# Three fp32r products instead of one fp32 product in an FFN, and layer-norm variances on VectorE

## The reference

```python
def _feature_map(x): return jax.nn.elu(x) + 1.0
# 1: linear attention, 16 heads of 16
q = _feature_map((n @ Wq + bq).reshape(B, S, H, Dh)); k = _feature_map(...); v = ...
kv = jnp.einsum('bkhd,bkhm->bhdm', k, v)
out = jnp.einsum('bqhd,bhdm->bqhm', q, kv) / normalizer[..., None]
x = x + out.reshape(B, S, D) @ Wo + bo
# 2: FFN with a shared expert, and routed ones
out_shared = _sq_relu(xf @ Ws1) @ Ws2            # 256 -> 128 -> 256
# 3: attention over the first 16 tokens of each batch, three iterations; every other row gets only the bias ob
out = attn_out @ ow.T + ob
# 4: the same FFN as in 2, with the same weights, on the new x
```

## Time and profile before

| | |
|---|---|
| median of 3 runs | 400.91 us |
| the profiled execution | 400.6 us |
| its span | 398.7 us |
| mean granted clock of PE | 0.992 of full speed |
| second pass, first to last L1163 | 182.93 to 378.46 us |

### The profile page before, as it was taken

How to read it: one execution, slowest core, us unless ns; L and a number is a source line. 1 busy time by engine, 2 the same in 40 slices (tenths; PEclk the granted TensorE clock), 3 DMA queues, 4 the chain that set the end, 5 groups by cost and what they waited for, 6 DMA issues and landing times.

```text
span 398.7 us, 7260 instructions
## 1 busy us (share of the span) xinstructions
PE 373.1 (94%) x2458; PEld 306.7 (77%) x2458; DVE 297.6 (75%) x677; ACT 234.2 (59%) x402; POOL 249.7 (63%) x305
## 2 busy tenths in 40 slices
PE   8879999999999999988879999999999998989993
PEld 4778989998999899876758887687667766677762
DVE  5688786778677866785696559887787879885574
ACT  3587776777677767544444755356454554364451
POOL 3388885788578855579373536787465845955302
PEclk9999999999999999999998999999999999999998
DMA  8831111111100000032530321233223321331103
GB/s 258 249 102 53 54 53 54 54 53 54 55 0 2 0 2 0 19 92 93 163 98 23 109 76 65 88 109 110 57 70 99 111 80 36 108 110 57 48 10 113
DMA packets 29625, 29.79 MB, mean 75 GB/s; under 512 B 5750, under 2 KB 25468, under 8 KB 29564
## 3 DMA queue, kind: packets, MB, share of 16 engines
q1 hardware_dynamic: 29004, 28.51, 23.3%
q10 hardware_dynamic: 560, 0.52, 0.5%
HBM read 19.98 MB, written 8.98 MB: 73 GB/s over the span
## 4 chain that ended last, share of the span: by engine, by line
PE 63%; DVE 18%; issue 7%; POOL 7%; ACT 3%; DMA 1%; DVEq 0%; POOLq 0%; ACTq 0%; SPq 0%
PE PB L1585 6%; DVE ln_bn L1109 5%; PE PA L1655 3%; PE PG L1436 3%; PE PA L1661 3%; PE PA L1656 3%; PE PG L1431 3%; PE PG L1432 3%; PE PT L1345 2%; PE PT L1632 2%; DVE x_all L1163 2%; DVE x_all L1171 2%; POOL o_lo L535 2%; PE PB L1390 2%; PE PA L1390 2%
## 5 line engine op out<-in xcount | busy, mean ns | idle before, releaser
L535 POOL TENSOR_TENSOR o_lo<-q_all,o_hi 128x512 fp32r<-128x512 f32 x32 | 40.2, 1279 | 33.5 <-ACT o_hi L811 33.5
L518 POOL TENSOR_TENSOR xn_pair<-scratch,xn_pair 128x512 fp32r<-128x512 f32 x32 | 41.9, 1308 | 30.6 <-ACT xn_pair L654 30.6
L1585 PE MATMUL PB<-ws,scratch 128*128 128x256 f32 x240 | 58.8, 388 | 1.6 <-DVE x_all L1171 1.5
L1585 PEld LDWEIGHTS PB<-ws,scratch 128*128 128x128 f32 x240 | 44.2, 192 | 15.4 <-issue 10.6
L1109 DVE BATCH_NORM_STATS2 ln_bn<-x_all 128x6 f32<-128x256 f32 x128 | 44.9, 413 | 0.9
L511 POOL TENSOR_TENSOR x_all<-x_all,wvo 128x1024 f32<-128x1024 f32 x16 | 45.3, 2833 | 0.0
L527 POOL TENSOR_TENSOR q_all<-q_all,scratch 128x512 f32<-128x512 f32 x32 | 41.3, 1313 | 0.0
L818 ACT ACTIVATE scratch<-PB,ln_rsq 128x256 f32<-128x256 f32 x28 | 11.7, 470 | 41.1 <-issue 25.9
L935 DVE TENSOR_TENSOR o_lo<-scratch,o_hi 128x512 fp32r<-128x512 f32 x32 | 32.8, 1024 | 4.1 <-ACT o_hi L672 2.7
L1431 PE MATMUL PG<-xn_pair,o_hi 128*128 128x256 f32 x128 | 32.1, 285 | 2.0 <-ACT o_hi L672 2.0
L647 ACT ACTIVATE scratch<-x_all,ln_shift,ln_rstd 128x255 f32<-128x255 f32 x60 | 31.0, 596 | 4.0 <-POOL ln_shift L507 4.0
(11 more groups left out here) (283 smaller groups left out, 1101.3 us busy)
## 6 DMA issues: line engine op xcount, KB each, us to landing
scratch<-inv_scratch SPq DMA_DIRECT2D x32, 256.0 KB
x_all<-n_L_attn_a_inputs_q_dram SPq DMA_DIRECT2D x15, 512.0 KB, 3.5
out_dram<-x_all SPq DMA_DIRECT2D x15, 512.0 KB, 5.7
inv_scratch<-inv_turned SPq DMA_DIRECT2D x16, 32.0 KB
out_dram<-x_all SPq DMA_DIRECT2D x2, 256.0 KB, 2.3
x_all<-n_L_attn_a_inputs_q_dram ACTq DMA_DIRECT2D x2, 128.0 KB, 2.8
x_all<-n_L_attn_a_inputs_q_dram SPq DMA_DIRECT2D x2, 128.0 KB, 2.9
setup<-in_L_attn_a_Wq_dram ACTq DMA_DIRECT2D x1, 256.0 KB, 4.9
```

The lines of the kernel that those rows point to most:

```text
L518: nc.gpsimd.tensor_tensor(halves[:, :, 1, :], pair(xn[n % 2], h), halves[:, :, 0, :].bitcast(F32), ALU.subtract).then_inc(x_lo, 1)
L535: nc.gpsimd.tensor_tensor(o_lo[:, c, :], q[:, c, :], o_hi[:, c, :].bitcast(F32), ALU.subtract).then_inc(o_lo_done, 1)
L1585: last = mm(four(dst)[:, t, :], h[:, t * P:(t + 1) * P], ws2[:, :], start=(t % 2 == 0 and not onto_rows), stop=True, skip_group_check=True)
```

## The change

The folded product and the first down projection become three fp32r products each. ACT makes `h2_hi` from `h2s` behind `lay_ob`, POOL `h2_lo` behind its addition L622, and `ws2` and `wc` are split once, in step 0. PE takes the high products behind the output product, and the low ones behind `chain(i, 3)`. The variances move from POOL to the end of DVE's step, with the reciprocal; the inverse norm stays at the head of DVE's next step. Two of the four statistics of L1163's result now stand behind the additions L1171. The second down projection stays fp32, and waits for each of its PSUM banks by itself.

```diff
@@ gpsimd, step
-                if runs(r) or runs(v):
-                    ge(pool, rsq, i - 1)
-                    variances(i, r, v)
                 if 1 <= i < B:
                     scale_query(i + 1)
                 chain(i, 1)
...
                     nc.gpsimd.tensor_tensor(last, last, y3[:, by_dve(v):T, :], ALU.add).then_inc(out_pool, 1)
+                if runs(r):
+                    pool.wait_ge(h2_hi_done, r + 1)
+                    ge(pool, f2_mm, 2 * r)
+                    nc.gpsimd.tensor_tensor(h2_lo[:, :], h2s, h2_hi[:, :].bitcast(F32), ALU.subtract).then_inc(h2_lo_done, 1)
                 chain(i, 2)
                 if i + 1 < NG:
                     query_low(i + 1)
@@ scalar, fold_ffn and fold_ffn_product
+                nc.scalar.activation(ws2_hi[:, :], ws2[:, :], ACT.Copy).then_inc(ws2_hi_done, 1)
...
-                nc.scalar.activation(wc, PT[:, 0, 0:F], ACT.Copy).then_inc(fold_sb, 1)
+                act.wait_ge(bo_added, NG)
+                nc.scalar.activation(wc_hi[:, :], PT[:, 0, 0:F], ACT.Copy).then_inc(fold_sb, 1)
@@ scalar, step
                     lay_ob(i, r, v)
+                    act.wait_ge(f1_scaled, r + 1)
+                    ge(act, f2_mm, 2 * r)
+                    nc.scalar.activation(h2_hi[:, :], h2s, ACT.Copy).then_inc(h2_hi_done, 1)
@@ vector
-            def reciprocal_variances(i, r, v):
...
+            def inverse_variances(i):
+
+                slots = slice(0 if runs(i) else 1, 2 if runs(i - 1) else 1)
+                a, d, both = ln_a[:, slots, :], ln_d[:, slots, :], ln_bn[:, slots, :, :]
+                ge(dve, rsq, i)
+                if runs(i):
+                    dve.wait_ge(bn2, T * (i + 1))
+                if runs(i - 1):
+                    dve.wait_ge(bn3, T * i)
+                nc.vector.tensor_tensor(d, both[:, :, :, 1], both[:, :, :, 4], ALU.subtract).then_inc(var, 1)
+                nc.vector.tensor_tensor(a, both[:, :, :, 2], both[:, :, :, 5], ALU.add).then_inc(var, 1)
+                dve.wait_ge(var, 5 * i + 1)
+                nc.vector.tensor_tensor(d, d, d, ALU.mult).then_inc(var, 1)
+                dve.wait_ge(var, 5 * i + 2)
+                nc.vector.tensor_scalar(a, a, 4.0 / D, 4.0 * LN_EPS, ALU.mult, ALU.add).then_inc(var, 1)
+                dve.wait_ge(var, 5 * i + 4)
+                nc.vector.tensor_tensor(a, a, d, ALU.add).then_inc(var, 1)
+                dve.wait_ge(var, 5 * i + 5)
+                ge(dve, r2_mm, i)
+                if runs(i - 1):
+                    ge(dve, f4_scaled, act_tiles(i - 1))
+                nc.vector.reciprocal(ln_rsq[:, slots, :], a).then_inc(rsq, 1)
@@ vector, step
+                    dve.wait_ge(ws2_hi_done, 1)
+                    nc.vector.tensor_tensor(ws2_lo[:, :], ws2[:, :], ws2_hi[:, :].bitcast(F32), ALU.subtract).then_inc(wc_lo_done, 1)
                 if i + 2 < NG:
                     inverse_norm(i + 2)
-                if runs(r) or runs(v):
-                    reciprocal_variances(i, r, v)
...
-                    x_stats(n, 0, bn2)
+                    x_stats(n, 0, bn2, (0, 1) if runs(r) else range(T))
                 if runs(r):
...
                                                 ALU.add).then_inc(f2_added, 1)
+                if runs(i) and runs(r):
+                    x_stats(n, 0, bn2, (2, 3))
                 chain(i, 3)
...
+                if i <= NG:
+                    inverse_variances(i)
@@ tensor
-            def down(dst, h, done, onto_rows):
+            def down(dst, h, done, free):
 
                 for t in range(T):
...
+                    if t % 2 == 0:
+                        ge(pe, f2_added, free + t // 2)
...
+            def inner_high(r):
+
+                pe.wait_ge(h2_hi_done, r + 1)
+                for w in (wc_hi, wc_lo):
+                    mm(PT[:, 0, :], w[:, :], h2_hi[:, :], start=False, stop=False, skip_group_check=True)
+
+            def down_high(r):
+
+                pe.wait_ge(ob_laid, r + 1)
+                for t in range(T):
+                    for w in (ws2_hi, ws2_lo):
+                        mm(four(PB)[:, t, :], h2_hi[:, t * P:(t + 1) * P], w[:, :], start=False, stop=False, skip_group_check=True)
+
+            def inner_and_down_low(r):
+
+                pe.wait_ge(h2_lo_done, r + 1)
+                mm(PT[:, 0, :], wc_hi[:, :], h2_lo[:, :], start=False, stop=True, skip_group_check=True).then_inc(f3_mm, 1)
+                for t in range(T):
+                    last = mm(four(PB)[:, t, :], h2_lo[:, t * P:(t + 1) * P], ws2_hi[:, :], start=False, stop=True, skip_group_check=True)
+                    if t % 2 == 1:
+                        last.then_inc(f2_mm, 1)
@@ tensor, step
                 if runs(r):
-                    pe.wait_ge(f1_scaled, r + 1)
-                    mm(PT[:, 0, :], wc, h2s, start=False, stop=True, skip_group_check=True).then_inc(f3_mm, 1)
+                    inner_high(r)
+                    down_high(r)
                 chain(i, 3)
                 if runs(r):
-                    pe.wait_ge(ob_laid, r + 1)
-                    down(PB, h2s, f2_mm, True)
+                    inner_and_down_low(r)
```

More of the change, by code:

```diff
@@ L170, in hybrid_kernel @@
         w1c = part(C * F).rearrange("p (c f) -> p c f", c=C)
-        wc = part(F)
         l_blk = [part(P) for _ in range(3)]
@@ L185, in hybrid_kernel @@
         kvt = [g[:, 0:C * P].rearrange("p (c n) -> p c n", c=C) for g in g_flat]
-        token_of = sb("token_of", [P, B * P])
+        ws2_hi, ws2_lo = sb("ws2_hi", [P, D], F32R), sb("ws2_lo", [P, D], F32R)
+        h2_hi, h2_lo = sb("h2_hi", [P, GT], F32R), sb("h2_lo", [P, GT], F32R)
+        wc_hi, wc_lo = sb("wc_hi", [P, F], F32R), sb("wc_lo", [P, F], F32R)
         PT, PA, PB, PG = ps("PT"), ps("PA"), ps("PB"), ps("PG")
@@ L219, in hybrid_kernel @@
         xs, xsub = used_q[1](D, SP), used_q[1](D, SP)
+        token_of = used_q[1](B * P)
         lin, kc, vi = [used_q[2](D, SP) for _ in range(3)]
@@ L277, in hybrid_kernel @@
         fold_mm, fold_sb, w1c_ready = [sem(n) for n in ("fold_mm", "fold_sb", "w1c_ready")]
+        ws2_hi_done, wc_lo_done, h2_hi_done, h2_lo_done = [sem(n) for n in ("ws2_hi_done", "wc_lo_done", "h2_hi_done", "h2_lo_done")]
         stored = sem("stored")
@@ L556, in _ @@
             routed = pool.value_load(routed_flag[0:1, 0:1], min_val=0, max_val=1)
[L558 to L574, removed]
             def run_experts(r):
@@ L1104, in run_experts, with x_stats @@
                         experts(2 * NG, SP, 1, lambda t: x_s_out.rearrange("p (t d) -> p t d", t=1), four(PB)[:, 2:3, :], h_s, 0)
-            def x_stats(n, slot, bn):
-                for t in range(T):
+            def x_stats(n, slot, bn, tiles):
+                for t in tiles:
                     nc.vector.bn_stats(ln_bn[:, slot, t:t + 1, :], x_tile(n, t)).then_inc(bn, 1)
-            def reciprocal_variances(i, r, v):
[L1113 to L1119, removed]
+            def inverse_variances(i):
[19 more added lines that the diff above has]
+                nc.vector.reciprocal(ln_rsq[:, slots, :], a).then_inc(rsq, 1)
             def scaled_sum(i, v, nv):
@@ L1176, in step @@
                     ge(dve, var, 5 * i)
-                    x_stats(nr, 1, bn3)
+                    x_stats(nr, 1, bn3, range(T))
                     run_experts(r, nr)
@@ L1580, in fold_ffn_product @@
                 last.then_inc(fold_mm, 1)
-            def down(dst, h, done, onto_rows):
+            def down(dst, h, done, free):
                 for t in range(T):
-                    last = mm(four(dst)[:, t, :], h[:, t * P:(t + 1) * P], ws2[:, :], start=(t % 2 == 0 and not onto_rows), stop=True,
-                              skip_group_check=True)
-                    if onto_rows and t % 2 == 1 or t == T - 1:
-                        last.then_inc(done, 1)
+                    if t % 2 == 0:
+                        ge(pe, f2_added, free + t // 2)
+                    last = mm(four(dst)[:, t, :], h[:, t * P:(t + 1) * P], ws2[:, :], start=(t % 2 == 0), stop=True, skip_group_check=True)
+                last.then_inc(done, 1)
+            def inner_high(r):
[14 more added lines that the diff above has]
+                        last.then_inc(f2_mm, 1)
             def row_scales(i):
@@ L1621, in step @@
                         pe.wait_ge(f4_scaled, act_tiles(v))
-                    else:
-                        pe.wait_ge(f2_added, 2 * (v + 1))
-                    down(f4_pair(v), h3, f4_mm, False)
+                    down(f4_pair(v), h3, f4_mm, 2 * v + 1 if v < NG - 1 else -1)
                 chain(i, 1)
@@ L1628, in step @@
                         pe.wait_ge(fold_sb, 4)
+                        pe.wait_ge(wc_lo_done, 2)
                     ge(pe, f3_relu, r)
@@ L1638, in step @@
                     pe.wait_ge(t2_done, C * NG)
-                    down(f4_pair(v), h3, f4_mm, False)
+                    down(f4_pair(v), h3, f4_mm, 0)
                 chain(i, 2)
```

3 lines of the change are left out of this document (added).

## The result

The changed kernel takes 405.74 us (median of 4 runs, 403.97 to 407.9) against 400.75 us before: 1.0149 of it, 95% interval 1.0103 to 1.0194. Measured again beside the experiments it was 405.46 us, 1.0134 (1.0103 to 1.0165). It is slower, by some 5 us; the forecast was 408.6. The profiled execution is the slowest of the first four (407.9 us, span 406.1), so I read sizes turn by turn and check them against the second profile (405.6 us, span 403.8).

A forecast was written before the change was run, and what follows sets the result against it. PE, busy 94%, bounds turns 4 and 6, but a loop over DVE sets the pace in turns 8, 11, 13 and the final stretch. Turn terms sum to +7.7: 400.6 + 7.7 + 0.3 = 408.6 us, range 399 to 414.

The forecast's parts named there:

- Products' price and turn 4: Folded and first down products: 2.04 us of issue instead of 2.59, 0.5 us a turn; PE-bound turn 4 keeps its 0.5.
- Steps 10 and 12: Subtraction waits behind POOL's power and L622; first addition at W (L1163's start) + 4.1, not 2.6; turns 11, 13 lose 1.2, 1.3.
- POOL's order: In POOL's queue the subtraction stands behind the link and L622, ahead of query_low; low part ready 5.8 us behind L1208.
- Turns 8 to 14 together: Sign to look for in the changed profile: these turns together 7.2 us longer; forecast wrong if no longer than before.
- Turn 8: In step 7 a power and L622 stand ahead of the subtraction; with the link's 0.9 us the turn loses 1.8.
- Inverse norm no longer hidden: L1005 to L1013 (1.5 us), hidden under POOL's variances, now follow them; links 0.9 us later, paid in turns 8, 9, 10, 12.
- Turns 1 to 3: ACT's copy ahead of m_high loses about 2 us, step 2's links no longer meet POOL: net -0.4, bounds -1.5 and +0.4.
- The end: Final stretch: variances give twice 0.5 us, the longer way takes all of the products' 0.5: -1.0.
- Turn 6: In step 5 a shorter link (0.85 us) and L622 stand in front of the subtraction: +1.4 us.
- The port once a turn, no worse than before: DVE's new two-input operations wait for L527 once a turn, no worse than before except turns 5, 7, 8 (up to 0.9 us).
- the second rival: POOL's next operation goes between DVE's small ones: one more L527 in eight turns, +7.6, 416 us; chance 0.10.
- The first rival: PE is the bound and the rest hides: seven turns of 0.5 us and more, -5.5, 395.4 us; chance 0.19.

The follow-up runs named there:

- the variances alone: The kernel before with nothing changed but the variances moved from POOL to DVE at the end of the step: 398.00 us, ratio 0.9948.
- the products alone: The changed kernel with the variances back on POOL and the inverse norm under them; new products and POOL's subtraction stay: 408.75 us, ratio 1.0192.
- copies unread: The kernel before with variances on DVE, plus ACT's copy and POOL's subtraction that nobody reads; PE keeps its old products: 403.64 us, ratio 1.0079.
- low products that read h2_hi: The changed kernel with low products reading h2_hi instead of h2_lo, so PE doesn't wait for POOL's subtraction: 402.43 us, ratio 1.0064.
- the end order: The changed kernel with POOL's subtraction ahead of its addition L604 in the last step alone: 406.09 us, ratio 1.0133.
- the order of m_high: The changed kernel with ACT's m_high ahead of the copy h2_hi in step 1: 405.90 us, ratio 1.0146.

## Why the prediction was right, and where it wasn't

The direction and the range held (408.6 forecast, 405.7 measured), by two errors that partly cancel, so the nearness of the number is luck in part. Put the forecast's terms in two heaps. The variances' share was the links' delay in turns 8, 9, 10 and 12 (+3.3), turn 5 (+0.5), turns 1 to 3 (-0.4), turn 15 and the end (-1.5): +1.9. It measured -2.1. The products' way, all the rest, was +5.8; from the variances alone to the changed kernel it measured +7.5.

- **Products' price and turn 4**: right. In step 10 the two L1605 start 0.23 us apart, in the last step the L1612 0.12; turn 4 lost 0.47 us (0.5 forecast), and with the products alone 0.46. Over the kernel it is little: from copies unread to low products that read h2_hi the ratio falls by 0.0015, inside the intervals. That step also holds PE's wait for the copy, the new order of the statistics and the waits bank by bank.
- **Steps 10 and 12**: the mechanism right, the turns half as dear. L1178 comes at W + 4.14 (W + 4.1), and the rows above have each link named. But turns 11 and 13 lost 0.6 and 0.7 us, where the forecast had 1.2 and 1.3. The variances alone gave 0.6 and 0.7 there; against them the changed kernel loses 1.2 and 1.4, and 0.7 and 0.9 with the copies unread, where PE waits for neither. So what I took for POOL's order alone is in part the port. In the changed kernel PE's wait has taken the block's place: DVE comes later and finds the port free.
- **Turns 8 to 14 together**: the forecast says 7.2 us, but its own terms add up to 7.6. They are 6.6 us longer in the first profile and 4.6 in the second, which has no lower clock in turn 8. Turns 9 and 14 lost 0.2 and 0.1 to 0.2 us each, where I had 0.9.
- **Turn 8** failed in its mechanism: +1.8 forecast, +1.3 measured at the full clock. The step had the low part wait in POOL's queue behind a power and L622. In step 7 L604 was done, and the subtraction waited for ACT's copy (POOL and DVE of the changed kernel's second profile; W is 274.23):

```profile
274.45 1.30 POOL L608 TENSOR_TENSOR h_lo<-scratch,h_hi 128x512 fp32r<-128x512 f32 x1 [0.65 <-ACT h_hi L848]
...
279.27 1.40 DVE L1100 BATCH_NORM_STATS2 ln_bn<-x_all 128x6 f32<-128x256 f32 x4
...
283.04 0.84 DVE L1132 SCALAR_TENSOR_TENSOR x_all<-PB,ln_rsq,x_all 128x256 f32<-128x256 f32 x2
```

  L1178 came at W + 2.6, as L1171 did before. The statistics end at W + 6.44 instead of W + 5.77, since two of them now stand behind the additions, and L1132 starts at W + 8.8 instead of W + 7.5: 0.7 us by the statistics' order and 0.6 by the inverse norm.
- **Inverse norm no longer hidden**: the mechanism right, the size not. The forecast had the links 0.9 us later. With the variances alone L1120 (L1128 of before) starts 0.6 us later in turns 8, 9 and 10, and these turns lose 1.3 us, not 2.7; turn 12 can't be read for the clock. The 3.3 us from moving it behind the link (2.6 with the products and the end order) equal the forecast's 3.3 by chance: they hold gains beyond the kernel before.
- **Turns 1 to 3** failed: -0.4 forecast (bounds -1.5 and +0.4), -2.6 measured, and -4.0 with the variances alone. The step said that the links of step 2 no longer meet POOL, and priced one operation of 1.27 us. It left out the three L1228 ahead of it (2.0 us) and credited PE's clock with nearly nothing.
- **The end** failed: -1.0 forecast, +2.2 measured. The step had the longer way take the products' 0.5 us and no more, but in the last step ACT's tiles come behind the copy, and POOL's L604 with them ahead of the subtraction. That is 1.8 of the 3.2 us by the end order's trace, half-speed down projection included.
- **Turn 6** failed: +1.4 forecast, -0.3 and +0.3 measured in the two profiles. I took step 5 for a short step 10. There the link and L604 are done 0.1 us ahead of W, PE waits 0.33 us for the subtraction, and L1178 starts at W + 2.05.
- **The port once a turn, no worse than before**: too low. In turn 7 it blocked three of the five operations, the second rival's mechanism, in both profiles (DVE and POOL of after):

```profile
266.07 1.01 DVE L1111 TENSOR_TENSOR ln_d<-ln_bn 128x8 f32<-128x8 f32 x1
...
267.01 2.52 POOL L530 TENSOR_TENSOR q_all<-q_all,scratch 128x512 f32<-128x512 f32 x2
267.11 1.20 DVE L1114 TENSOR_TENSOR ln_d<-ln_d 128x8 f32<-128x8 f32 x1
...
268.43 1.11 DVE L1118 TENSOR_TENSOR ln_a<-ln_a,ln_d 128x8 f32<-128x8 f32 x1
```

It happened in one turn and not in eight, so the 416 us did not come. The turn lost 1.1 and 0.6 us in the two profiles (0.6 forecast). The rival's condition, an L527 that begins more than 0.5 us later than before, does not decide it: in turn 11 L530 begins 1.2 us later, and nothing is blocked, as DVE comes later too.

- **The first rival** (PE is the bound, 395.4) fell: seven turns were to give 0.5 us, and turns 4 and 15 did (0.5 and 0.7, part of the latter by the variances).

What stays open: why turn 14 loses 0.6 us with the copies unread, and the 1.3 us of turn 1, which the order of m_high moves to turn 2 but doesn't remove.

## What to carry to other kernels

An operation on an idle engine isn't free because nobody waits for it: here the two added ones cost 5.3 us unread, for the larger part since they push that engine's next large operations beside another engine's small ones. Ask of each added or removed operation what stands behind it in its queue and what it will run beside, and price the removal as carefully as the addition. Split a change in its halves before believing a sum: this one was +7.5 and -2.1 us, and its better half, with three operations moved behind the link, is the fastest version here, 394.9 us.

## What the runs showed of the hardware

The changed kernel, with the same 1.74 us standstill of PE in turn 8, came out at the full granted clock in one profile and at 0.89 over the turn in the other, as in three kernels near to it; at the lower clock 128x256 products run 0.41 us instead of 0.28 for about 3.5 us, 1.5 us lost. In the kernel with the variances alone PE stood still for 0.55 and 1.80 us around its row scales in turn 12, and this window, from 333.0 on, shows the clock at 0.77, the turn 3.0 us longer than before:

```profile
333.00:340.40 7.40, 5.39 (x31) 5.18 (x32) 4.08 (x12) 2.82 (x5) 3.74 (x3) 0.77 0.19 62
```

Where the lower clock came, the turn lost 1.5 us beside the 1.74 of the wait itself, enough to make the times of one kernel scatter by more than 1 us. These standstills stand right ahead of it, but the profile that kept its clock had the same one, so it is not shown that they bring it.

Not every POOL operation holds up DVE: POOL's power (L583, 128x16, 2.91 us) ran beside DVE's L1269 in turn 7 of after, which reads two operands of 128x256 and took its usual 0.42 us, where POOL's 128x512 operations made 128x8 operations take up to 1.2 us instead of 0.17.
